# Layer 0 of a fused two-layer transformer kernel: more products of zeros at two turns on TensorE, and one group of moments issued ahead of a wait

## What is computed

```python
h = layernorm(x) * (1 + ca) + sa
# _L0_attn_ref
h = layer_norm(h, norm1_g, norm1_b)
q, k, v = split(h @ qkv_w.T)
q, k = elu(q) + 1, elu(k) + 1
kv, ksum = k.T @ v, sum(k)                    # per head
attn = (q @ kv) / (q @ ksum + 1e-6)
x1 = h_in + attn @ proj_w.T + proj_b
x1 = x1 + gelu(layer_norm(x1) @ fc1_w.T + fc1_b) @ fc2_w.T + fc2_b
x = x + ga * x1
# _L0_ffn_ref on h = layernorm(x) * (1 + cb) + sb
probs = softmax(h @ router_w.T)               # 16 routed experts, top 4
out = sum(gelu(h @ up[r].T) * gate[r] @ down[r].T) + shared experts
x = x + gb * out
```

## Time and profile before

| | |
|---|---|
| median of 3 runs | 2463.85 us (2462.29 to 2464.6) |
| the profiled execution | 2467.89 us; its span 2466.0 us |
| TensorE busy | 2296.2 us, 93% of the span |
| VectorE busy | 1740.9 us, 71% |
| ScalarE busy | 1285.7 us, 52% |
| GpSimd busy | 1385.0 us, 56% |
| mean granted TensorE clock | 0.954 of full |

### The profile page before, as it was taken

The page is one execution under the profiler, slowest core; times in us unless marked ns, Lnnn a source line. Parts: engine busy times, 40 slices in busy tenths (PEclk is TensorE's granted clock), DMA queues, the critical chain, the costliest instruction groups (busy, mean ns, idle before and its releaser), DMA issues.

```text
span 2466.0 us, 39735 instructions
## 1 busy us (share of the span) xinstructions
PE 2296.2 (93%) x10653; PEld 1363.7 (55%) x10654; DVE 1740.9 (71%) x4461; ACT 1285.7 (52%) x1712; POOL 1385.0 (56%) x751
## 2 busy tenths in 40 slices
PE   4989898599999999999999999999999997969995
PEld 2566565356565655555555555555556553437663
DVE  5687785477777777777777777877787864744444
ACT  1223322266666666666666666666666662314442
POOL 2121120177676768676767777777767684743221
PEclk7999898599999999999999999999999997989998
DMA  7001202100000000000000000000000002111114
GB/s 266 1 6 74 80 1 79 31 14 10 15 11 13 18 15 11 13 12 13 21 11 12 13 14 10 13 20 14 10 15 11 13 20 113 38 39 45 43 42 126
DMA packets 71231, 81.41 MB, mean 33 GB/s; under 512 B 18324, under 2 KB 56980, under 8 KB 71000
## 3 DMA queue, kind: packets, MB, share of 16 engines
q1 hardware_dynamic: 66808, 71.58, 9.2%
q0 software_dynamic: 4352, 8.99, 1.1%
HBM read 49.97 MB, written 32.66 MB: 34 GB/s over the span
## 4 chain that ended last, share of the span: by engine, by line
PE 86%; DVE 6%; issue 3%; POOL 2%; SPq 1%; DMA 1%; ACT 1%; POOLq 0%; DVEq 0%; ACTq 0%
PE P L1774 18%; PE P L1738 12%; PE P L1759 9%; PE P L1760 9%; PE P L1725 5%; PE P L1596 3%; PE P L1969 3%; PE P L1973 3%; PE P L1610 3%; PE P L1992 3%; PE P L1781 2%; PE P L1792 2%; PE P L1707 2%; PE P L1743 1%; PE P L1982 1%
## 5 line engine op out<-in xcount | busy, mean ns | idle before, releaser
L1393 ACT ACTIVATE big<-P 128x1024 f32<-128x1024 f32 x512 | 511.9, 1020 | 188.4 <-PE P L1760 84.5
L998 DVE CUSTOM_DVE_ANT_0 big<-P,near 128x512 f32<-128x512 f32 x512 | 349.0, 682 | 231.4 <-PE P L1738 231.2
L1774 PE MATMUL P<-big,V 128*64 128x512 f32 x2048 | 481.3, 602 | 0.0
L601 POOL TENSOR_TENSOR spair<-spair,big 128x1024 f32<-128x1024 f32 x192 | 456.9, 2380 | 13.2
L601 POOL TENSOR_TENSOR opair<-opair,big 128x1024 f32<-128x1024 f32 x192 | 456.6, 2378 | 13.8 <-ACT big L1393 0.6
L1738 PE MATMUL P<-Ka,Qa 96*128 96x512 f32 x1024 | 451.8, 463 | 4.8 <-DVE mhalf L998 3.3
L1001 DVE TENSOR_REDUCE mhalf<-P 128x1 f32<-128x512 f32 x512 | 349.2, 682 | 85.9 <-PE P L1738 75.9
L1759 PE MATMUL P<-Qa,Ka 97*128 97x512 f32 x1024 | 408.4, 399 | 0.5 <-ACT big L1393 0.5
L1760 PE MATMUL P<-Qb,Kb 128*128 128x512 f32 x1024 | 406.5, 397 | 0.0
L1738 PEld LDWEIGHTS P<-Ka,Qa 96*128 96x128 f32 x1024 | 185.9, 191 | 224.4 <-issue 118.6
L588 POOL TENSOR_TENSOR big<-big,sinv 128x512 f32<-128x512 f32 x64 | 81.8, 1279 | 378.5 <-DVE sinv L973 378.5
(11 more groups left out here) (288 smaller groups left out, 3483.8 us busy)
## 6 DMA issues: line engine op xcount, KB each, us to landing
slots<-later SPq DMA_DIRECT2D x4, 4224.0 KB, 13.8
Ka<-auxrows SPq DMA_DIRECT2D x66, 128.0 KB, 2.2
big<-in_wex SPq DMA_DIRECT2D x8, 768.0 KB, 9.0
xt<-slots SPq DMA_DIRECT2D x76, 66.0 KB, 1.8
wqk<-in_whead SPq DMA_DIRECT2D x66, 64.0 KB, 1.8
near<-in_aux SPq DMA_DIRECT2D x66, 64.0 KB, 1.8
big<-yrows SPq DMA_DIRECT2D x8, 512.0 KB, 7.2
hT<-hkeep SPq DMA_DIRECT2D x5, 512.0 KB, 3.8
```

The lines of the kernel that those rows point to most:

```text
L601: pool.tensor_tensor(psum8[s][:, :], psum8[s][:, :], pfull[:, j % RING, :], ALU.add).then_inc(S["p_added"], 1)
L998: dve.tensor_tensor_reduce(scratch, P[:, 6 + i, :], near[s][:, left:left + HALF], -1.0, 3.0e38, ALU.add, ALU.min, mhalf[:, i, t:t + 1]).th ...
L1393: act.activation(pfull[:, j, :], banks(2 * (j % 2)), ACT.Exp, scale=DH1 ** -0.5).then_inc(S["exp_done"], 1)
L1774: mm = pe.matmul(P[64 * i:64 * i + 64, 4, :], V1[:, j, s, :], half(pfull[:, j, :], i), start=(j == 0), stop=(j == T - 1))
```

## The change

Three edits, all in layer 0. At the outputs' turn, 2 products of zeros into bank 4 ahead of the wait for each half, 3 ahead of the first half's in batches 1 to 3. At the turn for the experts, for b > 0, 6 products of zeros in place of 2 between the turns `c1` and `b0`; in all batches 4 between the halves of `b0` and 5 in place of 4 behind it. On VectorE, for b > 0, the 4 BN_STATS of the second half of `c0` go between Q's `min` and the wait for its exponential; the BN_AGGR and the add stay where they were. The arithmetic of the result is the same.

```diff
+            def half_stats(tag, i, src):
+                s = tag[0] == "c"
+                for t in range(i * TPH, (i + 1) * TPH):
+                    dve.bn_stats(statss[s][:, t, :], src[:, t, :]).then_inc(S["ln_moments"], 1)
...
                 dve.tensor_scalar(A[:, 0, :], banks(0), 0.0, None, ALU.min).then_inc(S["q0_min"], 1)
+                if b > 0:
+                    half_stats(f"c0{b - 1}", 1, tok(xs[:, b - 1, :]))
                 dve.wait_ge(S["q0_exp"], b + 1)
...
                 if b > 0:
-                    c_moments(b - 1, 1)
+                    half_moments(f"c0{b - 1}", 1, tok(xs[:, b - 1, :]), False)
...
-            def turn(tag, bank, src=xn):
+            def turn(tag, bank, src=xn, between=0):
                 for t in range(T):
+                    if t == TPH and between:
+                        keep_busy(4, between)
...
                 for i in range(NHALF):
+                    keep_busy(4, 3 if i == 0 and b > 0 else 2)
                     pe.wait_ge(S["o0_tok"], EACH["o0_tok"] * b + i + 1)
...
-                keep_busy(2, 10 if b == 0 else 2)
-                turn(f"b0{b}", 2)
-                keep_busy(4, 4)
+                keep_busy(2, 10 if b == 0 else 6)
+                turn(f"b0{b}", 2, between=4)
+                keep_busy(4, 5)
                 copied(f"b0{b}")
```

More of the change, by code:

```diff
@@ L675, in _, with half_moments @@
             cst = A[:, 0:5, :].rearrange("p a b -> p (a b)")
-            def half_moments(tag, i, src):
+            def half_stats(tag, i, src):
+                s = tag[0] == "c"
+                for t in range(i * TPH, (i + 1) * TPH):
+                    dve.bn_stats(statss[s][:, t, :], src[:, t, :]).then_inc(S["ln_moments"], 1)
+            def half_moments(tag, i, src, stats_too=True):
+                if stats_too:
+                    half_stats(tag, i, src)
                 s = tag[0] == "c"
                 nth = NHALF * LN_TAGS[tag] + i
-                for t in range(i * TPH, (i + 1) * TPH):
-                    dve.bn_stats(statss[s][:, t, :], src[:, t, :]).then_inc(S["ln_moments"], 1)
                 dve.wait_ge(S["ln_moments"], (2 * nth + 1) * TPH)
```

## The result

| | before | changed |
|---|---|---|
| median of 6 runs | 2464.18 us | 2449.95 us |
| lowest to highest | 2462.29 to 2465.82 | 2448.34 to 2454.67 |
| profiled execution, its span | 2467.89, 2466.0 | 2451.34, 2449.5 |
| mean granted clock | 0.954 | 0.963 |

The changed kernel is faster: ratio 0.9945, 95% interval 0.9932 to 0.9958, or 14.2 us. The forecast was 2446.4 us and 17.5 us. The measured median lies 0.45 us above the prediction's own range of 2443.5 to 2449.5, and inside the reach to 2453 that it gave for falls in one batch or two.

A forecast was written before the change was run, and what follows sets the result against it. TensorE holds 86% of the chain, at half clock around the outputs' and experts' turns. Savings 4.2 + 13.8 = 18.0, less 0.5 for starts not lining up, 17.5 us: 2463.85 - 17.5 = 2446.4 us, range 2443.5 to 2449.5.

The forecast's parts named there:

- the reach to 2453: Forecast range extended to take in clock falls in one batch or two; within it chance 0.09 of the time.
- The turn for the experts: Layer 0, all batches: clock holds through turn and router's products; 3.45 us saved per batch, 13.8 in four.
- The BN_STATS: VectorE, batches 1 to 3: their 0.86 us fit the 1.12 us wait for Q's exponential, at zero cost.
- The outputs' turn: Layer 0, batches 1 to 3: earlier transposes and projection at full clock; 1.40 us per batch, 4.2 in three.
- the 0.53 us: Part of the outputs' turn: projection at full clock cuts VectorE's first residual's wait from 1.85 to 1.32 us.
- The reading of the clock: Busy shares rising to 85% (outputs' turn) and 87% (experts' turn), like batch 3's `a2`, would hold the clock.
- its own signs: Wrong if any 0.50 stretch stays between 90 and 400 us, or the gates' turn waits for ScalarE's gelus.
- The rival in which the clock falls at the experts' turn all the same: Clock still falls at the experts' turn, only the outputs' turn gains; 2461.4 us, chance 0.06.
- a fall behind the router's products: Rival: clock falls later; 2456 to 2460 us, or 2450 to 2455 if in one or two batches; together 0.10.

The follow-up runs named there:

- e3_no_out_products: Changed kernel without the 2 or 3 products of zeros at the outputs' turn; 2450.77 us, ratio 0.9946 to the kernel before.
- e8_stats_only: Kernel before with only the BN_STATS moved ahead of Q's combination, no products added; 2479.83 us against 2484.76, ratio 0.9981.
- e4_more_a2: Changed kernel with 17 products of zeros instead of 14 ahead of turn `a2` in batches 1 to 3; 2449.45 us, ratio 0.9938 to the kernel before.
- e7_four_behind: Changed kernel with 4 products of zeros instead of 5 behind the experts' turn; 2471.12 us against 2483.25 for the kernel before, ratio 0.9956.
- e1_experts: Changed kernel with only the experts' turn edits, outputs' turn and BN_STATS as before; 2453.09 us, ratio 0.9957 to the kernel before.

## Why the prediction was nearly right

**The turn for the experts** was right in mechanism and size. 3.56, 3.52, 3.24 and 3.44 us were saved, 13.8 in all, as the sum had it. The two terms of it were a little off and made up for each other in batch 1: the router's products started 0.67 us earlier after fc2, not 0.6, and 7.78 us passed from there to the gates, not 7.65. The router's products took 1.93 us instead of the assumed 1.85, and from the first step of VectorE's chain to the gates' turn it was 192.24 - 186.43 = 5.81 us against 5.75: TensorE and VectorE arrive nearly together, since the last step of VectorE's chain ends at 191.80 + 0.29 and the gates' turn starts at 192.24. Of the added products only those between the halves were shown to be needed.

**The BN_STATS** went under the wait as forecast; the combination's wait fell from 1.12 to 0.34 us, where the text said about 0.2. Two pairs of kernels give 2.3 and 4.9 us for the move, both compatible with 2.6; in the second the profile shows that the move also kept the projection at full clock.

**The outputs' turn** had the step that failed: "VectorE has no idle time from there to the turn `a2` and almost none to fc2's residual, so nothing gives it back". The norms did come 1.4 us earlier in batch 1: the residual's wait was 1.32 us. (That the five products of zeros brought the 0.53 us of it isn't shown: the clock stayed up there without them, see e3_no_out_products and e8_stats_only.) But the 14 products of zeros, which at the low clock had ended with the norms, ended 0.83 us before them at the high one. The text noted that they end "before the norms are there, as in batch 0" and costed it at nothing. With that wait and the paced transposes of `a2` behind it (each waits for its tile's norm), the clock fell at the start of fc1 in batches 1 to 3 of the profiled execution, which made fc1 1.0 to 1.2 us longer. So TensorE gave back what VectorE had gained: the term was 1.0 us instead of 4.2. With 17 products in place of 14 K to fc2 was 1.3 us shorter per batch. In another execution of the changed kernel two of the three falls didn't come, and the term was 3.7; with no fall at all it was 5.0 (e4_more_a2, e7_four_behind, e8_stats_only), more than forecast, since the 0.53 us was read in batch 1 and the low clock had cost more in batches 2 and 3 (K to fc2 35.62 and 35.72 us before, against 35.32). So the term is worth between 1 and 5 us, by the execution. That the wait ahead of `a2` makes the falls is what the 17 products show (none in 11 turns, against 18 in 36). Why the clock falls in some of these turns with the wait and not in others stays open.

**The reading of the clock** was wrong in kind. The prediction took the busy share of single stretches of one execution for what decides. But stretches with the same share went both ways: 60% (2.22 of 3.70 us, batch 0's turn for the experts) fell in the kernel before and stayed up in `e8_stats_only`; 71% (2.42 of 3.40, the turn `a2`) fell in the changed kernel and stayed up in `e7_four_behind`; 40% (1.63 and 1.64 of 4.10, the outputs' turn) fell in the kernel before and stayed up in `e1_experts`. The first of these was in the trace of the kernel before already: a fall after a larger share than the 48% that batch 0's outputs' turn had kept its clock with. That more work in such a stretch makes a fall rarer is what the counts above show; when one comes depends on the execution.

The Trainium skill ("TensorE: Matmul & The Clock Gate", Part 1) says that the chip's count of TensorE's activity runs freely and doesn't start anew with the kernel, and that the number of slow products at a kernel's start varies from run to run for that reason. It says this of the start; the pairs of executions here would fit it in mid-kernel, but no run moved a stretch against that count on purpose. The Trainium skill's rule of Part 4 on the same page, on transposes that don't count as busy the same way, remains untested: in all thin stretches here transposes and waits come together. Filling the waits was enough, with the transposes as they were.

By its own signs the prediction was wrong in one thing: it named any stretch of 0.50 left between 90 and 400 us, and there were three. The rival in which the clock falls at the experts' turn all the same came in no execution of the changed kernel that was profiled, nor did a fall behind the router's products. The 1.8 us that layer 1 gave in the profiled execution were forecast by nothing; without them the profiled spans would differ by 14.7, which is close to the medians' 14.2. That the total came within 3.3 us of the forecast is due to the experts' term, which was right. The outputs' term was short by 3.2 us in that execution and by 0.5 in the other, so how near the medians came to the forecast is in part luck.

## What to carry to other kernels

When products of zeros keep TensorE's clock up, follow what comes next at the new speed: filler (the products of zeros) that was counted out at the low clock ends early at the high one and opens a wait further on. Put the filler where the wait is, between the halves of a paced turn rather than only ahead or behind, and enough that the wait nearly closes; here the time then also varied less from run to run (3.2 us over six runs against 7.2). Don't read from one execution that a stretch keeps or loses the clock: compare versions by many runs, and count the falls over many turns. And try each piece of filler by itself: here the two or three products at the outputs' turn were of no use that shows.

## What the runs showed of the hardware that was not expected

The same instructions with the same busy time kept 2.4 GHz in one execution and fell to 1.2 GHz in another (batch 0 of the kernel before and of the one with the BN_STATS alone, 10.1 us at 0.50 or none). The same was seen at the outputs' turn, where the clock once stayed up after 1.64 us of work in 4.10, and at `a2`. With four products of zeros, 0.22 us apart, between the halves of the experts' turn, and others ahead and behind, the clock stayed up in 36 of 36 turns, against 3 of 16 without the four. The length of the low stretch at the start of layer 1 was 61.3 us in the kernel before and 57.9 us in the changed one, for the same work. And across the runs of a kernel the mean granted clock and the time go together: for the changed kernel 0.965 with 2448.3 to 2449.0 us, 0.963 with 2450.9 and 2451.3, 0.962 with 2454.7.
